# Layer norms of a transformer tower: high parts before squares, centring before low parts, statistics between the low products

## What is computed

```python
def _layernorm(x, axis=-1, eps=1e-05):
    m = jnp.mean(x, axis=axis, keepdims=True)
    v = jnp.var(x, axis=axis, keepdims=True)
    return (x - m) / jnp.sqrt(v + eps)

h = _L0_tok_ref(L0_tok_A_abslog, L0_tok_A_phase, x, 1024)
h = h + _L0_attn_ref(_layernorm(h), Wq, Wk, Wv, Wo)       # 1024x1024 each
h = h + _L0_ffn_ref(_layernorm(h), w_idx, absmax, bias)   # 1024x1024
h = h + _L1_attn_ref(_layernorm(h), W_in, ..., W_out)     # state-space layer, inner width 2048
h = h + _L1_ffn_ref(_layernorm(h), W_base, b_base, W_router, A, B)   # base product, top-2 of 8 LoRA experts
```

## Time and profile before

| | us |
|---|---|
| median of three runs (lowest, highest) | 4201.65 (4200.85, 4206.2) |
| the profiled execution | 4200.29 |
| its span in the profile | 4198.1 |
| TensorE busy | 3953.9 (94%) |
| VectorE busy | 2749.8 (66%) |
| ScalarE busy | 2035.5 (48%) |
| GpSimd busy | 2169.8 (52%) |
| granted TensorE clock, mean over the span | 0.977 |

### The profile page before, as it was taken

The page is one execution under the profiler, slowest core; times in us unless marked ns, Lnnn a source line. Parts: engine busy times, 40 slices in busy tenths (PEclk is TensorE's granted clock), DMA queues, the critical chain, the costliest instruction groups (busy, mean ns, idle before and its releaser), DMA issues.

```text
span 4198.1 us, 58597 instructions
## 1 busy us (share of the span) xinstructions
PE 3953.9 (94%) x22408; PEld 2595.2 (62%) x22408; DVE 2749.8 (66%) x3026; ACT 2035.5 (48%) x2976; POOL 2169.8 (52%) x912
## 2 busy tenths in 40 slices
PE   5899999999999999899999999999999999989998
PEld 1568777444768777444577867644377877734466
DVE  6955553999355563799635564499925556289943
ACT  7832345777232344677423234577633224477732
POOL 0033343888534333788633334488843343388852
PEclk7999999999999999999999999999999999999999
DMA  4242233000322233100222223200132222300021
GB/s 114 76 145 71 81 116 106 12 15 15 120 91 80 77 100 114 45 15 15 67 104 92 82 74 124 84 15 15 37 105 96 81 86 101 112 23 15 15 84 69
DMA packets 93813, 303.21 MB, mean 72 GB/s; under 512 B 11521, under 2 KB 15873, under 8 KB 91009
## 3 DMA queue, kind: packets, MB, share of 16 engines
q1 hardware_dynamic: 80320, 275.70, 19.9%
q10 hardware_dynamic: 13248, 24.12, 1.8%
HBM read 255.74 MB, written 44.04 MB: 71 GB/s over the span
## 4 chain that ended last, share of the span: by engine, by line
PE 52%; issue 28%; DVE 9%; POOL 9%; ACT 1%; POOLq 0%; DMA 0%; DVEq 0%; ACTq 0%
PE psg L929 20%; PE psx L1175 10%; POOL sb_wl L524 9%; PE psg L1190 8%; DVE sb_wst L1731 7%; PE psg L999 3%; PE psg L1204 2%; PE psg L1004 1%; PE psg L1152 1%; PE psx L1217 1%; PE psg L1201 1%; PE psg L1162 1%; DVE psg L1704 1%; PE psg L1302 1%; DVE psg L1703 1%
## 5 line engine op out<-in xcount | busy, mean ns | idle before, releaser
L524 POOL TENSOR_TENSOR sb_wl<-sb_raw,sb_wh 128x1024 fp32r<-128x1024 f32 x388 | 962.1, 2484 | 1816.0 <-ACT sb_wh L635 1815.7
L1731 DVE TENSOR_TENSOR_SCAN sb_wst<-sb_dA,psx 128x1024 f32<-128x1024 f32 x512 | 1140.1, 2271 | 36.7 <-ACT sb_dA L771 23.7
L1175 PEld LDWEIGHTS psx<-sb_dgB,sb_duT 64*128 64x128 f32 x4096 | 358.7, 189 | 525.8 <-DVE sb_wst L1731 260.0
L771 ACT ACTIVATE sb_dA<-sb_dlt,sb_a_sb 128x504 f32<-128x504 f32 x1024 | 646.4, 705 | 61.3 <-DVE sb_wst L1731 55.7
L1175 PE MATMUL psx<-sb_dgB,sb_duT 64*128 64x256 f32 x4096 | 591.0, 408 | 85.6 <-DVE sb_wst L1731 83.8
L635 ACT ACTIVATE sb_wh<-sb_raw 128x1024 fp32r<-128x1024 f32 x388 | 407.4, 1053 | 530.0 <-PE psg L929 238.5
L557 POOL TENSOR_TENSOR sb_wst<-sb_wst,sb_cb_lo 128x1024 f32<-128x1024 f32 x256 | 599.5, 2364 | 89.8 <-DVE sb_wst L1731 89.8
L557 POOL TENSOR_TENSOR sb_wst<-sb_wst,sb_cb_hi 128x1024 f32<-128x1024 f32 x256 | 598.4, 2359 | 75.5 <-DVE sb_wst L1731 75.5
L1190 PE MATMUL psg<-sb_wst,sb_cst 64*64 64x512 f32 x4096 | 557.7, 617 | 10.3 <-POOL sb_wst L557 9.6
L929 PE MATMUL psg<-sb_xh,sb_wh 128*128 128x512 f32 x2080 | 533.5, 399 | 12.6 <-POOL sb_wl L524 7.1
L929 PE MATMUL psg<-sb_xh,sb_wl 128*128 128x512 f32 x2080 | 516.7, 390 | 0.0
(11 more groups left out here) (279 smaller groups left out, 5083.5 us busy)
## 6 DMA issues: line engine op xcount, KB each, us to landing
sb_raw<-in_w SPq DMA_DIRECT2D x360, 512.0 KB, 3.5
sb_raw<-w_ffn_dequantized SPq DMA_DIRECT2D x32, 512.0 KB, 3.2
gates<-sb_gt ACTq DMA_DIRECT2D x64, 256.0 KB, 2.4
sb_gin<-gates SPq DMA_DIRECT2D x64, 256.0 KB, 2.7
h_after_tok<-sb_h SPq DMA_DIRECT2D x4, 2048.0 KB, 8.7
sb_h<-h_after_tok SPq DMA_DIRECT2D x4, 2048.0 KB, 7.9
out<-sb_h SPq DMA_DIRECT2D x4, 2048.0 KB, 7.2
sb_dqi<-in_w_idx ACTq DMA_DIRECT2D x28, 256.0 KB, 4.1
```

Of the source, the lines that this page charges most:

```text
L524: pool.tensor_tensor(rest(b, i0), raw[:, i0 % RAW, :, :], high(b, i0).bitcast(F32), ALU.subtract).then_inc(s_wl, 1)
L771: ins_ = A(dA[:, (m * NQ + k) % RING, :, n, 1:S], dlt[:, m % 2, :].rearrange("p (b s) -> p b s", b=NB)[:, :, 1:S], ACT.Exp, scale=a_sb[:, ...
L1175: ins_ = mm(psx[:, 2 * j + r, :].rearrange("p (a t e) -> p a t e", a=8, e=2)[:, :, :, e], duT[r0:r0 + 64, m % 2, i * P:(i + 1) * P], dgB[r ...
L1731: v.tensor_tensor_scan(wst[:, x, 4 * j:4 * j + 4, :, :].rearrange("p b n s -> p (b n s)"), dA[:, x, 4 * j:4 * j + 4, :, :].rearrange("p b ...
```

## The change

In ACT's norm all eight high parts come first and all eight squares after them. In DVE's norm all eight centrings come first and all eight low parts after them. On TensorE all `highs` of a pair come first; the two sums of squares, which stood inside and behind the highs, now stand before the lows and after six of them, and `variance` moves from behind four lows to behind twelve. In the last layer the first sum of squares goes behind the highs, the second behind the router's product, and `variance` behind the eight lows of LA0 rather than behind four. Norm L = 0 of blocks 1 to 3 has no centring in `norm`, so that there only ACT's and TensorE's orders change.

```diff
@@ ScalarE, norm
                     A(xh[:, k, :], xc[:, k, :], ACT.Copy).then_inc(s_xh, 1)
+                for k in range(KC):
                     A(sq[:, k, :], xc[:, k, :], ACT.Square).then_inc(s_sq, 1)
@@ TensorE, strip_pair
                 for k in range(KC):
                     highs(k)
-                    stat(b, L, k)
-                lows(0, range(4))
+                stat(b, L, 3)
+                lows(0, range(6))
+                stat(b, L, 7)
+                lows(0, range(6, KC))
+                lows(1, range(4))
                 variance(b, L)
-                lows(0, range(4, KC))
-                lows(1, range(KC))
+                lows(1, range(4, KC))
@@ TensorE, last layer
-                        stat(b, 3, k)
+                    stat(b, 3, 3)
                     settle(pe)
 
                     for k in (0, 4):
                         ins_ = over_tiles(2, lambda n: wr[:, n, :], lambda n: xc[:, n, :], k)
                     ins_.then_inc(s_rout, 1)
+                    stat(b, 3, 7)
                     for k in range(KC):
                         pe.wait_ge(s_xl, b * LNU + 3 * KC + k + 1)
-                        if k == 4:
-                            variance(b, 3)
                         ins_ = mm(psg[:, 3, :], wh[:, slot(b, LA0), k, :], xl[:, k, :], start=False, stop=(k == KC - 1))
@@
+                    variance(b, 3)
                     for k in range(KC):
                         ins_ = mm(psg[:, 0, :], wh[:, slot(b, BASE0), k, :], xl[:, k, :], start=False, stop=False)
@@ VectorE, norm
                     for k in range(KC):
                         centre(b, L, k)
-                        if k >= 2:
-                            low(k - 2)
-                    low(KC - 2)
-                    low(KC - 1)
+                    for k in range(KC):
+                        low(k)
```

## The result

The changed kernel takes **4228.94 us** (median of 5 runs, 4224.09 to 4232.86) against 4201.33 (5 runs of the kernel before, 4200.81 to 4206.2): ratio 1.0062, 95% interval 1.0049 to 1.0076. It is slower by 27.6 us. The forecast was 4209.0 with a range from 4202.5 to 4215, and "within 0.2%" its likeliest outcome; rival B gave 4225.

A forecast was written before the change was run, and what follows sets the result against it. TensorE, busy 94% of the span, was taken to wait for `rstd` behind the pairs; 14.5 - 1.2 - 1.3 - 3.7 = +8.3 us on 4200.29 gave 4208.6, taken as 4209.0, range 4202.5 to 4215.

The forecast's parts named there:

- rival B: Eight longer waits in QKV and WIN each also drop the clock: +24.8 us, 4225; chance 0.10.
- ACT's and DVE's order: FFN norms of blocks 1 to 3: TensorE no longer waits for late high parts, -1.2 us.
- Nothing elsewhere: Outside the full-clock FFN norms of blocks 1 to 3, the new ACT and DVE order gains nothing.
- The narrow runs: Last layer: first sum of squares joins the router's run, saving 0.3 us a block, -1.3 us in four.
- The late variance: QKV and WIN: `rstd` comes eight lows later, lengthening eight waits by 1.81 us each, +14.5 us.
- The covers of FFN and of the last layer: Slack behind the variance, 2.9 us in the last layer and two strips (10.9 us) in FFN: delay costs nothing.
- The clock: Half-clock stretches: last layers -4.8, block 3 -1.6, one FFN fall +1.1, one longer wait +1.6; together -3.7 us.
- the eight longer waits: TensorE's waits at strip 2 (QKV, block 0), strip 3 (QKV, blocks 1 to 3), strip 4 (four WIN): each +1.81 us.
- near 4214: The time given if only three or four of the eight longer waits drop the clock.
- C: QKV of blocks 1 to 3: `rsin` runs faster and gives back 1.8 us each, -5.4; total +2.9, 4203; chance 0.14.
- D: Highs were the bound at each entry and late `rstd` costs nothing: -12 us, 4188; chance 0.06.

The follow-up runs named there:

- 11: The changed kernel with fitted filling products (results overwritten) at the ways in and before WOUT, and repeated products ahead of seven longer waits: 4199.30 us, 0.9992.
- 10: The kernel before with fitted filling products (results overwritten) around the mean, in the last layer's router wait and before WOUT: 4186.59 us, 0.9961.
- experiment 1: The kernel before with only the variance of the QKV, FFN and WIN pairs moved behind twelve lows: 4229.12 us, 1.0062.
- Experiment 3: The changed kernel with eight products computed twice ahead of strip 3's wait (QKV, blocks 1 to 3) and strip 4's (WIN): 4228.29 us, 1.0067.
- 8: The changed kernel with too much filling at the ways in (three or four products each side of the mean) and repeats ahead of seven waits: 4224.31 us, 1.0046.
- the filled pair: The kernel before and the changed kernel, both with filling that fits, the changed one also with repeated products: 4186.59 and 4199.30 us.
- experiment 4: The kernel before with ACT's and DVE's new order alone, TensorE's order as before: 4222.81 us, 1.0048.
- experiment 5: The changed kernel with QKV's and WIN's sums after high 5 and variance before high 7, FFN's variance behind four lows: 4198.04 us, 0.9987.

## Why the prediction was wrong

**ACT's and DVE's order (forecast -1.2, FFN of blocks 1 to 3): nearly right.** FFN to WIN is shorter by 0.25 to 0.28 us in blocks 1 to 3, -0.8. "Nothing elsewhere" was right only because the clock was at half there: at full clock (11 against 10) there is a gain in all FFN norms, 0.3 us in WIN and some 0.3 us in the last layer too.

**The narrow runs (forecast -1.3): right.** Last layer to QKV is shorter by 0.40 to 0.46 us in three blocks, the last layer of block 3 by 0.26, 1.6 in all. At full clock (11 against 10) it is shorter by 0.74, of which some 0.3 are the highs, which no longer wait there.

**The late variance (forecast +14.5): right.** The list of waits says +13.1: 1.79 and 1.74 us each in QKV, 1.50 in WIN, where some 0.3 us more stand at the fourth strip (experiment 1). At full clock QKV pays 1.82 us, the eight lows of the estimate, and WIN 1.33 + 0.32 (what its pair gained) = 1.65, or 1.85 with the estimate for the scan. The covers of FFN and of the last layer held: FFN shows a gain and no wait.

**The clock (forecast -3.7): the step that failed, in sign and in size.** The order alone, from the table: 4 x (1.82 - 0.25 + 1.33 - 0.74) = +8.6 us. The span grew by 29.7. So some 21 us are left for the clock, a difference and not a measurement of its own, and by stage they are: QKV 3 x 1.53 and 3.9 in block 0 (5.72 less 1.82), together 8.5; WIN to the last layer 4.18 - 1.33 = 2.85 in block 1 and 3.1, 2.7 and 2.8 in blocks 0, 2 and 3, together 11.4; last layer about 0.3 a block, where the gain of the order was run at half clock. Of WIN's 2.85, about 1.6 stand behind the wait at strip 4, 0.65 at WOUT (92.70 us from its first product to the last layer before, 93.36 now) and 0.4 in the pair, which took its gain at half clock. Of block 0's 3.9, some 1.4 stand in the pair, whose way in kept half clock 3.4 us longer, and the rest behind the wait at strip 2.

The forecast asked only how the existing stretches at the ways in might move, and put one fall at one of the eight longer waits (+1.6). All eight fell, and none of the hoped-for gains came: the four last layers kept 6.8 us, block 3 kept its own. The price of one was right, 1.5 us for 3.4 us of half clock where it can be read alone (QKV of blocks 1 to 3). The number of them was wrong. What misled me was FFN of block 1, with two gaps of 1.5 and 1.6 us and full clock: I read it as "such gaps may or may not fall", and gave a single gap of 2.8 to 3.9 us the same doubt. The traces say otherwise. At these eight places, over all kernels run, a wait of 2.7 to 3.9 us was followed by half clock 19 times of 19 (eight in the changed kernel, eight in experiment 1, and the unfilled one of block 0 in 3, 8 and 11), and a wait of 1.0 to 2.1 us 0 times of 61. Between 2.1 and 2.7 us nothing was measured at these places. Experiment 3 shows that it is this idle time and not the delay: with the delay kept and the gap cut to 1.3 us in QKV and 1.0 us in WIN, seven of seven stretches went. (The repeats shorten the idle time by adding work ahead of it; the two were not told apart.)

The Trainium skill ("TensorE: Matmul & The Clock Gate", section "HAM oscillation — how this bites in real kernels") says that gaps between dense bursts bring half clock back, and that such a stretch costs half its length. The stretches in QKV of blocks 1 to 3 agree, with 1.5 us for 3.4. The prediction named the rule, and gave the case that follows from it a chance of 0.10.

**The rivals.** B said: idle at eight places grows and each drops the clock, +24.8, 4225. That is what happened, 4228.94; what it lacked are the stretches at WOUT (2.6 us) and the longer ones in block 0. Experiment 1, without those at WOUT, is its purest form: +26.7 us. The prediction's "near 4214" for a fall at three or four of the eight does not follow from B's own terms, which give 12.0 + 3.5 x 1.6 on 4200.3, near 4218. C fell: `rsin` takes 2.74 us as before. D fell: the waits grew, and the late variance alone makes a loss of the same size.

**The total.** Waits and order as predicted would have given +12.0 (14.5 - 1.2 - 1.3); the filled pair differs by 12.7 us (4199.30 - 4186.59), but that agreement is partly chance, as about 4 of it are clock and 8.6 the order. In the kernels without filling the same order costs 27.6.

**Still open.** Why WOUT's entry falls in the changed kernel and not in the one before (the gap there is 1.55 us in both), why the way into FFN falls in some kernels and not in others, and why the one into WIN falls for 3.4 us in some and for 6.8 in others, is not settled; I only saw that they do so with no edit near them.

## What to carry to other kernels

Price a longer wait of TensorE by two terms, its length and the half clock behind it, and look in the trace for the longest gap between dense strips that still kept the clock: here waits up to 2.1 us did at all eight places and those from 2.7 us never did. A chain of statistics whose result releases a later strip belongs ahead of products that have slack, even if it costs TensorE a little; moving it eight products back, and nothing else, cost 26.7 us, about half of it in waits and half in clock. Where a gap cannot be closed, a few products whose result is overwritten keep the clock, if they end before what they wait for arrives (0.9961 on the kernel before, 0.9925 with the early variance); with three products too many at each way in that gain was gone (1.001).

## What the runs showed of the hardware

The filling is made of plain float32 products with a constant weight. Each takes two records and 0.9 us (three take 2.73 us), against 0.23 us for a product of the strips. So one product more or less decides in a gap of 1.5 us.

The same gap gives half clock in one kernel and full clock in another: the way into FFN of block 1, with its two gaps of 1.5 and 1.6 us, ran at full clock in the kernel before and in the changed one, lost 3.4 us in experiment 4 and 6.8 us in experiment 5. Totals of one kernel scatter by some us, up to 4195.8 to 4209.5 for the kernel before in one group of 25 runs; that these places are the reason was not shown. The time up to the first high product of block 0, ahead of which hardly any edit lies, was 237.9 to 242.1 us in the profiled executions of the seven kernels without filling at the ways in, so a difference of 4 us between two profiles can come from there alone.
